# Attention values weighed in bursts of four heads, with eight transposed-probability buffers

## What is computed

```python
q = (xn @ Wq).reshape(b, n, H, DH).transpose(0, 2, 1, 3) * scale
k, v = split(xn @ Wkv)                        # one head each, shared by the 16 query heads
k, v = concatenate([null_k, k]), concatenate([null_v, v])     # a null key and value ahead
sim = einsum('bhid,bjd->bhij', q, k) + bias   # bias: 16 x 512 x 512, and a column for the null key
sim = where(causal_mask | padding, -max, sim)
attn = softmax(sim, axis=-1)
out = einsum('bhij,bjd->bhid', attn, v)
x = x + layernorm(out @ Wo)
```

## Time and profile before

| | |
|---|---|
| median of 3 runs | 1877.23 us (1870.98 to 1877.26) |
| the profiled execution, its own time | 1879.36 us |
| its span, first to last instruction | 1877.3 us |
| mean granted clock of TensorE | 0.94 of full speed |
| busy: PE, PEld, DVE, ACT, POOL | 90%, 73%, 55%, 38%, 42% |
| attend stage | 288 to 875 us of the span |

### The profile page before, as it was taken

How to read it: one execution, slowest core, us unless ns; L and a number is a source line. 1 busy time by engine, 2 the same in 40 slices (tenths; PEclk the granted TensorE clock), 3 DMA queues, 4 the chain that set the end, 5 groups by cost and what they waited for, 6 DMA issues and landing times. The chain is left out here.

```text
span 1877.3 us, 37692 instructions
## 1 busy us (share of the span) xinstructions
PE 1684.0 (90%) x10388; PEld 1374.0 (73%) x10389; DVE 1040.0 (55%) x3148; ACT 721.6 (38%) x1884; POOL 782.8 (42%) x1459
## 2 busy tenths in 40 slices
PE   6899967999999999997988894499999998999998
PEld 5677756887877877876777773387777886888886
DVE  5444445786776776775455555643333343455555
ACT  2222215676676666765122221033333343221221
POOL 1000326676686676774455555422222221223323
PEclk9999987998999998998999996599999999999999
DMA  6566659697787877783333333334565332223423
GB/s 228 177 228 219 218 170 250 166 228 164 166 214 179 182 201 159 200 199 94 115 134 132 129 130 150 158 99 169 184 226 210 106 106 91 87 93 123 145 90 112
DMA packets 220248, 301.83 MB, mean 161 GB/s; under 512 B 15201, under 2 KB 128401, under 8 KB 218082
## 3 DMA queue, kind: packets, MB, share of 16 engines
q1 hardware_dynamic: 189986, 235.20, 43.5%
q0 software_dynamic: 11280, 35.99, 6.4%
q10 hardware_dynamic: 18864, 29.38, 4.5%
HBM read 187.26 MB, written 113.26 MB: 160 GB/s over the span
## 5 line engine op out<-in xcount | busy, mean ns | idle before, releaser
L789 ACT ACTIVATE probs<-scores,lowest 128x514 f32<-128x514 f32 (+3 forms) x512 | 281.9, 555 | 25.5 <-DVE lowest L716 24.8
L688 POOL TENSOR_SCALAR probs<-probs,rsums 128x512 f32<-128x512 f32 (+3 forms) x512 | 264.9, 523 | 0.0
L716 DVE CUSTOM_DVE_ANT_0 scores<-psum,resident 128x514 f32<-128x514 f32 (+3 forms) x512 | 245.8, 489 | 25.7 <-issue 19.9
L842 PE MATMUL psum<-ident,probs 128*128 128x128 f32 x1280 | 249.9, 294 | 9.1 <-POOL probs L688 8.9
L831 PE MATMUL psum<-keys,queries 128*128 (+4 forms) x640 | 230.8, 369 | 27.5 <-DMA queries_and_ones<-q_hi_d 19.6
L858 PE MATMUL psum<-probsT,v_now 128*64 128x128 f32 x2560 | 205.2, 290 | 9.8 <-DVE probsT L730 7.2
L842 PEld LDWEIGHTS psum<-ident,probs 128*128 128x128 f32 x1280 | 149.7, 143 | 63.4 <-issue 35.4
L831 PE MATMUL psum<-keys_lo_and_mask,queries_and_ones 128*128 (+4 forms) x640 | 192.6, 310 | 0.0
L797 ACT ACTIVATE probsT<-psum 128x128 f32<-128x128 f32 (+3 forms) x256 | 111.9, 437 | 186.5 <-PE psum L842 184.1
L858 PEld LDWEIGHTS psum<-probsT,v_now 128*64 128x64 f32 x2560 | 139.2, 140 | 52.8 <-issue 34.8
L730 DVE COPY probsT<-psum 128x128 f32<-128x128 f32 (+3 forms) x256 | 125.3, 489 | 84.6 <-PE psum L842 79.9
(11 more groups left out here) (221 smaller groups left out, 3813.8 us busy)
## 6 DMA issues: line engine op xcount, KB each, us to landing
ys_d<-y_out ACTq DMA_DIRECT2D x72, 256.0 KB, 2.0
q_hi_d<-q_hi SPq DMA_DIRECT2D x64, 256.0 KB, 2.6
q_lo_d<-q_lo SPq DMA_DIRECT2D x64, 256.0 KB, 2.9
queries<-q_hi_d SPq DMA_DIRECT2D x32, 512.0 KB, 5.3
queries<-q_lo_d SPq DMA_DIRECT2D x32, 512.0 KB, 7.4
queries_and_ones<-q_hi_d SPq DMA_DIRECT2D x32, 512.0 KB, 9.3
oT_d<-o_out SPq DMA_DIRECT2D x64, 256.0 KB, 5.3
o_in<-oT_d SPq DMA_DIRECT2D x32, 512.0 KB, 3.8
```

The source lines that it names most:

```text
L688: pool.tensor_scalar(out=row, in0=row, scalar1=rsums[:, n % RING:n % RING + 1], scalar2=1.0, op0=ALU.mult, op1=ALU.mult).then_inc(probs_sc ...
L716: dve.tensor_tensor_reduce(out=scores[n % 4][:, 0:CK[i]], in0=score_psum(i, n), in1=bias_of(resident, i, h), scale=1.0, scalar=3.0e38, op0 ...
L789: act.activation(probs[n % RING][:, 0:CK[i]], scores[n % 4][:, 0:CK[i]], ACT.Exp, bias=lowest[:, n % 4:n % 4 + 1], scale=-1.0, accum_out=s ...
L842: last = pe.transpose(probsT_bank[n % 2][:, j * P:(j + 1) * P], probs[n % RING][:, AHEAD + j * P:AHEAD + (j + 1) * P], ident[:])
```

## The change

`weigh_values` takes four units at once instead of two, `probsT` has eight buffers instead of four, and the semaphore `pairs_weighed` becomes `bursts_weighed`, with one count for four units. At n % 4 == 1 PE weighs units n - 5 to n - 2, so its order is transpose, score four times over and then one burst of weighing. DVE's add_null moves from n % 8 == 2 to n % 8 == 3, which is behind that step's copy. On POOL the copy of v_now moves from n == 2 to n == 4 and the split of weights from n % 8 == 4 to n % 8 == 6. The two small operations of lines 686 and 715 are replaced by increments of semaphores that nobody waits for.

```diff
-        probsT = [sb(f"probsT{i}", [P, S]) for i in range(4)]
+        probsT = [sb(f"probsT{i}", [P, S]) for i in range(2 * BURST)]
...
             def scale(b, n):
                 if n % 2 == 0:
                     pool.wait_ge(rsums_ready, PB * b + n // 2 + 1)
-                    pool.tensor_tensor(out=waited[:, n // 2 % 4:n // 2 % 4 + 1], in0=ident[0:1, 0:1], in1=ident[0:1, 0:1], op=ALU.mult)
+                    pool.sem_inc(scaling_begun, 1)
...
                     scale(b, n)
-                    if n == 2:
+                    if n == 4:
                         if not (isinstance(b, int) and b == 0):
-                            pool.wait_ge(pairs_weighed, PB * b)
+                            pool.wait_ge(bursts_weighed, GB * b)
...
-                    if n % HALF == 4 and n // HALF < WC:
+                    if n % HALF == 6 and n // HALF < WC:
                         split_weights(b, n // HALF)
...
                     dve.wait_ge(probs_ready, UB * b + n - 3)
-                dve.memset(spare["dve"][:, n % 2:n % 2 + 1], 0.0)
+                dve.sem_inc(bias_begun, 1)
                 dve.tensor_tensor_reduce(out=scores[n % 4][:, 0:CK[i]], in0=score_psum(i, n), in1=bias_of(resident, i, h),
...
                 dve.wait_ge(probsT_full, UB * b + n + 1)
-                if not (isinstance(b, int) and b == 0 and n < 4):
-                    dve.wait_ge(pairs_weighed, PB * b + n // 2 - 1)
-                dve.tensor_copy(probsT[n % 4][:, 0:CK[n // H] - AHEAD], probsT_bank[n % 2][:, 0:CK[n // H] - AHEAD]
+                if not (isinstance(b, int) and b == 0 and n < 2 * BURST):
+                    dve.wait_ge(bursts_weighed, GB * b + n // BURST - 1)
+                dve.tensor_copy(probsT[n % (2 * BURST)][:, 0:CK[n // H] - AHEAD], probsT_bank[n % 2][:, 0:CK[n // H] - AHEAD]
...
-                dve.wait_ge(pairs_weighed, PB * b + HALF // 2 * (k + 1))
+                dve.wait_ge(bursts_weighed, GB * b + HALF // BURST * (k + 1))
...
                         copy_probs(b, n)
-                    if n % HALF == 2:
+                    if n % HALF == 3:
                         if n > HALF:
                             add_null(b, n // HALF - 1)
...
-            def weigh_values(b, m):
-                i, k = 2 * m // H, 2 * m // HALF
-                pe.wait_ge(probsT_even, PB * b + m + 1)
-                pe.wait_ge(probsT_odd, PB * b + m + 1)
+            def weigh_values(b, g):
+                i, k = BURST * g // H, BURST * g // HALF
+                pe.wait_ge(probsT_even, PB * b + BURST // 2 * (g + 1))
+                pe.wait_ge(probsT_odd, PB * b + BURST // 2 * (g + 1))
...
+                for n in range(BURST * g, BURST * (g + 1), 2):
+                    cols = slice(n % HALF // 2 * P, (n % HALF // 2 + 1) * P)
+                    for j in range(i + 1):
+                        for head in range(2):
+                            last = pe.matmul(o_bank[k % 2][head * DH:(head + 1) * DH, cols], v_now[:, j * DH:(j + 1) * DH],
+                                             probsT[(n + head) % (2 * BURST)][:, j * P:(j + 1) * P],
+                                             start=(j == 0), stop=(j == i))
+                last.then_inc(bursts_weighed, 1)
...
                         score(b + 1, n + LEAD - UB)
-                    if n % 2 == 0:
-                        if n:
-                            weigh_values(b, n // 2 - 1)
+                    if n % BURST == 1:
+                        if n > BURST:
+                            weigh_values(b, n // BURST - 1)
                         elif not first:
-                            weigh_values(b - 1, PB - 1)
+                            weigh_values(b - 1, GB - 1)
```

More of the change, by code:

```diff
@@ L532, in stage_attend @@
                  wo_loaded):
-    RING, LEAD = 8, 7
+    RING, LEAD, BURST = 8, 7, 4
     with ExitStack() as ctx:
@@ L552, in stage_attend @@
         probs = [sb(f"probs{i}", [P, AHEAD + S]) for i in range(RING)]
-        probsT = [sb(f"probsT{i}", [P, S]) for i in range(4)]
+        probsT = [sb(f"probsT{i}", [P, S]) for i in range(2 * BURST)]
         sums, rsums = sb("sums", [P, RING]), sb("rsums", [P, RING])
-        waited = sb("waited", [1, 4])
         v_now = sb("v_now", [P, TB * DH])
@@ L571, in stage_attend @@
         rsums_ready, probs_scaled = sem("rsums_ready"), sem("probs_scaled")
-        v_ready, pairs_weighed, o_ready = sem("v_ready"), sem("pairs_weighed"), sem("o_ready")
+        bias_begun, scaling_begun = sem("bias_begun"), sem("scaling_begun")
+        v_ready, bursts_weighed, o_ready = sem("v_ready"), sem("bursts_weighed"), sem("o_ready")
         o_stored = [sem(f"o_stored{i}") for i in range(2)]
@@ L578, in stage_attend @@
         PB = UB // 2
+        GB = UB // BURST
         HB = UB // HALF
@@ L794, in copy_probs @@
                 act.wait_ge(probsT_full, UB * b + n + 1)
-                if not (isinstance(b, int) and b == 0 and n < 4):
-                    act.wait_ge(pairs_weighed, PB * b + n // 2 - 1)
-                act.activation(probsT[n % 4][:, 0:CK[n // H] - AHEAD], probsT_bank[n % 2][:, 0:CK[n // H] - AHEAD], ACT.Copy
+                if not (isinstance(b, int) and b == 0 and n < 2 * BURST):
+                    act.wait_ge(bursts_weighed, GB * b + n // BURST - 1)
+                act.activation(probsT[n % (2 * BURST)][:, 0:CK[n // H] - AHEAD], probsT_bank[n % 2][:, 0:CK[n // H] - AHEAD], ACT.Copy
                                ).then_inc(probsT_even, 1)
@@ L844, in transpose_probs @@
                 last.then_inc(probsT_full, 1)
-            def weigh_values(b, m):
-                i, k = 2 * m // H, 2 * m // HALF
-                pe.wait_ge(probsT_even, PB * b + m + 1)
-                pe.wait_ge(probsT_odd, PB * b + m + 1)
-                if m == 0:
+            def weigh_values(b, g):
+                i, k = BURST * g // H, BURST * g // HALF
+                pe.wait_ge(probsT_even, PB * b + BURST // 2 * (g + 1))
+                pe.wait_ge(probsT_odd, PB * b + BURST // 2 * (g + 1))
+                if g == 0:
                     pe.wait_ge(v_ready, b + 1)
-                if m % (HALF // 2) == 0 and not (isinstance(b, int) and b == 0 and k < 2):
+                if BURST * g % HALF == 0 and not (isinstance(b, int) and b == 0 and k < 2):
                     pe.wait_ge(o_ready, HB * b + k - 1)
[L855 to L860, removed]
+                for n in range(BURST * g, BURST * (g + 1), 2):
[6 more added lines that the diff above has]
+                last.then_inc(bursts_weighed, 1)
             def body(b, first=False, last=False):
@@ L882, in _ @@
             body(B - 1, last=True)
-            weigh_values(B - 1, PB - 1)
+            weigh_values(B - 1, GB - 1)
 def stage_output(nc, x, cond, wo_stage, wo_loaded, g_out, wt, wg, dram, psum, ident, pow_half, eps, spare, logits):
```

## The result

The changed kernel takes 1929.74 us (median of 4 runs, 1929.31 to 1932.13), where the kernel before, run alongside, takes 1875.35 us. The ratio is 1.029, with a 95% interval of 1.027 to 1.0311: 54 us slower, where 81 were forecast. The profiled execution took 1929.49 us, its span 1927.5, at a mean granted clock of 0.946 (0.940 before).

A forecast was written before the change was run, and what follows sets the result against it. TensorE's own instructions and the chain through ACT and DVE set the attend stage's pace. Burst waits of 9.9 us in each of 8 batches, plus 7 x 1.0, less 5, add 81 us: 1958 us, range 1868 to 2025.

The forecast's parts named there:

- Fewer changes of kind: TensorE's changes into and out of weighing: half of 256 weighings go, 128 x 0.33 = 42 us saved.
- The chain: Within a burst, TensorE through ACT and DVE to the last score: 3.65 us against 3.12, 0.53 us wait in row 3.
- 0.91 us a burst in row 1, and half of that in row 0: Burst waits in shorter rows: row 1 chain 2.47 us against 1.56, so 0.91; row 0 taken as 0.45.
- add_null: On DVE behind copy(b), in the chain of every second burst: 0.67 us each, 0.33 a burst on average, 43 us.
- The turn: At the loop's turn, weighing moves behind TensorE's wait for add_bias: 1.0 us at each of 7 turns, replacing the burst's wait.
- The small operations: Memset on DVE and product on POOL become increments: 5 us won, bounds 8 lost and 15 won.
- GpSimd's moves: v_now's copy and the weight split moved later on POOL: covered by its idle 194 us, no separate cost.
- The first: Rival: the chain fits and the 42 us saving remains, 1830 to 1840 us, say 1833; chance 0.14.
- the second: Rival, near balance: waits at half size and add_null hidden in DVE's idle time, 1877 us; chance 0.08.
- The third: Rival: recurring waits keep TensorE's clock low, row 1 at 1.2 GHz in all batches, 60 us more, 2018 us; chance 0.12.
- The signs: Expected profile: 32-load weighings, scores waiting some 100 us for DVE, row 3 bursts about 6.2 and 6.9 us, 3 us turn idle.

The follow-up runs named there:

- Experiment 11: Experiment 7 with product and memset kept, GpSimd's split of expert weights cut to 8 of 512 columns (wrong weights): 1839.68 us.
- 10: The kernel before, with GpSimd's split of expert weights cut to 8 of 512 columns (wrong weights): 1862.56 us.
- experiment 4: The changed kernel with VectorE's copy ahead of its reciprocal at odd steps: 1919.14 us.
- Experiment 7: The changed kernel, bursts weighed at n % 4 == 0, add_null at n % 8 == 4, v_now's copy at n == 2: 1873.55 us; with product and memset 1870.38.
- experiment 3: The changed kernel with add_null back at n % 8 == 2: 1903.55 us.
- experiment 6: The kernel before, weighing in pairs, with add_null alone moved to n % 8 == 3: 1878.40 us.
- experiment 9: The changed kernel with a batch's last burst weighed at step 0 of the next, ahead of the score that waits: 1918.86 us.
- experiment 8: The changed kernel with GpSimd's two moves undone (v_now's copy at n == 2, split at n % 8 == 4): 1946.51 us.
- experiments 1 and 2: The first: the kernel before with increments in place of product and memset, 1880.58 us. The second: the changed kernel with product and memset back, 1927.18 us.

## Why the prediction was right, and which of its terms were not

Direction and range hold, and so does the mechanism in the main: bursts make TensorE wait for VectorE's bias, and 1930 us lie 28 below the forecast of 1958. That the sum came so near is in part luck, since errors of both signs stand in it. By its own steps:

- **Fewer changes of kind, 42 us saved.** Right as far as shown. Idle time ahead of weighing loads fell by 32 us, and a burst has one idle 0.17 us behind it for 32 loads. In row 3 the size is as forecast: a burst takes 6.70 us (670.53 to 677.23), of which 1.01 are wait, and 5.69 is 0.31 under two pairs of 3.00. Experiment 11 against 10 gives 22.9 us net, with the turn and what is left of GpSimd's waits in it. No run has the 42 us alone.
- **The chain, 0.53 us a burst in row 3.** Right for the burst: 3.59 us measured against 3.65, 0.47 of wait. The terms are off one by one and cancel: transposition to copy 0.69 for 0.79, reciprocal to copy 0.09 for 0.17, bias to score 0.87 for 0.75. The step n = 55 grew by 0.21 us, and 0.53 less 0.33 is 0.20; but n = 47 shrank by 0.25. Two things were not in it. VectorE's own sequence of bias, reciprocal, copy and bias is as long as the path through ScalarE, so that freeing the copy from the reciprocal gave 11 us and not 40 (experiment 4); and a part of the wait lies at the fourth transposition. Experiment 7 gets rid of 56 us (59 with product and memset), with add_null's place and the turn in them.
- **0.91 us a burst in row 1, and half of that in row 0.** The term that was most wrong. Over seven batches the steps n = 19 to 31 grew by 12 us where the terms give 26. A burst of row 1 without add_null comes to its last score after 2.29 us, not 2.47, and the waits lie ahead of its third score and its fourth transposition:

```profile
636.03 0.21 PEld L843 LDWEIGHTS psum<-ident,probs 128*128 128x128 f32 x2 [0.17 <-issue]
...
637.43 0.19 PEld L832 LDWEIGHTS psum<-keys,queries 128*128 128x128 f32 x1 [0.27 <-DVE lowest L717]
...
638.04 0.20 PEld L843 LDWEIGHTS psum<-ident,probs 128*128 128x128 f32 x2 [0.31 <-issue]
...
638.32 0.19 PEld L832 LDWEIGHTS psum<-keys,queries 128*128 128x128 f32 x1
```

It takes 3.86 us to the next burst (639.89), where two pairs of 1.72 us less 0.33 plus 0.91 are 4.02. The base failed as well: I had read one quick pair and taken it for the row. In the kernel before, the pairs from 601.12 to 606.94 take 1.84, 2.11 and 1.87 us, one of them with a wait for GpSimd's scale; and those from 608.66 on 1.89, 1.94 and 1.88, since from unit 25 on their scores are the wider ones of row 2:

```profile
605.07 0.20 PEld L842 LDWEIGHTS psum<-ident,probs 128*128 128x128 f32 x2 [0.61 <-POOL probs L688]
...
610.55 0.20 PEld L842 LDWEIGHTS psum<-ident,probs 128*128 128x128 f32 x2 [0.17 <-issue]
```

So two pairs are 3.65 to 4.01 us (steps n = 19, 23, 27), not 3.44. In row 0 the cheap half was still too much: over seven batches n = 3 to 15 grew by 0.7 us where the terms give 13, and n = 7 got 0.34 us shorter.
- **add_null, 43 us.** Right in kind, too large: 26 us net by experiment 3, 30 in the steps that hold it, and nothing in pairs by experiment 6. The eight steps that hold it grew by 4.6 us a batch where the terms give 7.9.
- **The turn, 1.0 us.** Too small: 2.5 us on average, of which experiment 9 gets 1.56 back. It is 2.9 us at the five turns by the loop's jump and 0.5 to 0.6 at the two others, where the prediction had 1.0 at each of seven. At the turn of 612 us the 32 loads take 1.25 us more than in row 3, and part of them runs at 1.2 GHz, behind an idle stretch. The prediction moved them behind the wait and priced them as if at full clock, though it had the low clock behind the turn in the earlier trace rows.
- **The small operations, 5 us won.** Wrong in sign: 4.1 us lost in pairs, and 2.6 in bursts, which is not clear of noise; inside the bounds given. The 30 us of memsets that were to leave VectorE didn't leave its busy time.
- **GpSimd's moves, nothing.** Wrong. They are worth 17 us (experiment 8). That idle time covers them was read from a sum over the stage; the cover lacks where batches begin.

Over the seven batches the eight steps with add_null were forecast at 56 us and took 31, the seven others at 17 and took 2, and the turns at 5 (1.0 less 0.33 saved, seven times) and took 16. That is 25 and 15 us too dear and 11 too cheap; less the 5 us that the small operations were to give, 24 of the 27 us by which 81 is over 54.

**The rivals.** The first (42 us faster) and the second (no change) are out by the time, and the waits of 73.8 us say why. The third is too: TensorE waits in the bursts of 631 to 690 us, rows 1 to 3, and the granted clock there is 1.00 (the windows' last row); only behind the turn is it low, 0.72 and 0.60 here, as it was before.

**The signs.** Groups of 32 loads with 0.17 us behind them came as written. Scores were to wait some 100 us and more for VectorE and waited 73.8, in 122 waits for 128 bursts. Bursts of row 3 were to take 6.2 and 6.9 us: 6.69 with add_null (n = 51), 5.86 without (n = 55), or 5.44 (n = 47). At n = 55 the kernel before takes 5.65 and not 6.00, because the last of its scores are the narrow ones of the next batch. TensorE was to be idle 3 us at the turn: 2.68, and 0.72 before it.

What stays open: how the 0.17 us of an increment come about, and why the loop's turn is longer with increments; how much of the change of the seven ordinary steps outside row 3 is saving and how much wait; and what the weighing's place alone is worth, with add_null left where it was.

## What to carry to other kernels

Work that looks like a cost (a change of kind in the middle of a stream) may be the cover of a round trip through other engines; before joining such pieces, sum the round trip against what is left between them, and choose the step at which the joined piece lies by where the trip's long link is: one step, with add_null moved along, was worth 56 us here. Take the base of a sum from the mean of a row of the trace and not from its quickest pair. And price work that moves behind an idle stretch at the clock which the trace shows there.

## What the runs showed of the hardware

- An increment of a semaphore that ends a wait is not free beside a tiny operation: the bias started 0.50 us behind the matmul's start with it and 0.32 to 0.33 with a 59 ns memset (experiments 1 and 2), and a kernel with 768 such increments took 4.1 us longer, by longer turns of the loop.
- A turn by the hardware loop's jump took 5.5 to 6.1 us in the kernel before, and one into or out of written-out batches 3.9, between the same two copies.
- The 32 loads of a weighing take 1.90 us at full clock and 3.15 us at the turn, behind 3 us in which TensorE was busy for 0.40; in ordinary bursts, whose longest single wait was 0.9 us, the granted clock stayed at 1.00 (631 to 690 us).
